# Message passing in graph layers on one Trainium2 core: edge stage with edges as rows, an addition on VectorE and paired transposes

## What is computed

```python
x = layernorm(x + L0(x))   # normalised aggregation, @W, relu
x = layernorm(x + L1(x))   # x @ U.T + segment_sum(x[src], dst) @ V.T, relu
x = layernorm(x + L2(x))   # mean aggregation, concatenated with x, @W
x = layernorm(x + L3(x))
# L3, for every edge (src, dst):
h = relu(concat(x[src], x[dst]) @ W1 + b1)
interaction = h @ W2 + b2
gate = sigmoid(interaction @ Wg + bg)
pooled = segment_sum(interaction * gate, src) / max(count, 1)
```

## Time and profile before

| | us |
|---|---|
| median of 3 runs | 5006.15 (4980.84 to 5015.29) |
| profiled execution, its own time | 5014.18 |
| its span, first to last instruction | 5012.5 |
| PE busy in the span | 4088.1 (82%) |
| DVE busy | 2211.0 (44%) |
| ACT busy | 1761.9 (35%) |
| POOL busy | 1593.1 (32%) |

### The profile page before, as it was taken

The page is one execution under the profiler, slowest core; times in us unless marked ns, Lnnn a source line. Parts: engine busy times, 40 slices in busy tenths (PEclk is TensorE's granted clock), DMA queues, the critical chain, the costliest instruction groups (busy, mean ns, idle before and its releaser), DMA issues.

```text
span 5012.5 us, 126263 instructions
## 1 busy us (share of the span) xinstructions
PE 4088.1 (82%) x39351; PEld 3185.7 (64%) x39352; DVE 2211.0 (44%) x6640; ACT 1761.9 (35%) x3887; POOL 1593.1 (32%) x1694
## 2 busy tenths in 40 slices
PE   6873688888798999968988998788788888897895
PEld 3442344444598989846776776666666776676674
DVE  9998899999604030232222222222222222222224
ACT  7861588888400000122222222222222222222222
POOL 0000100000001010165555555555555555555553
PEclk9985899999899999956567656767777667767767
DMA  1000122222597979611111111111111111111111
GB/s 39 4 2 9 64 112 103 103 103 114 217 346 261 344 264 338 234 37 38 38 38 40 39 40 38 37 39 40 37 39 39 38 40 39 39 40 38 38 41 33
DMA packets 182786, 443.67 MB, mean 89 GB/s; under 512 B 52923, under 2 KB 111555, under 8 KB 176159
## 3 DMA queue, kind: packets, MB, share of 16 engines
q1 hardware_dynamic: 131503, 387.98, 22.4%
q0 software_dynamic: 51040, 53.55, 5.4%
q10 hardware_dynamic: 144, 1.05, 0.1%
HBM read 356.29 MB, written 86.12 MB: 88 GB/s over the span
## 4 chain that ended last, share of the span: by engine, by line
PE 46%; DVE 14%; another core or an unknown queue 12%; issue 10%; ACTq 6%; DMA 6%; ACT 4%; DVEq 1%; POOL 1%; SPq 0%; PEldq 0%; POOLq 0%
PE ps L1528 9%; PE ps L1636 8%; DVE x L542 7%; PE ps L1658 7%; PE ps L1646 7%; PE ps L1633 7%; PE ps L1499 6%; DMA rows<-adjacency 5%; DVE rows L696 3%; ACTq L1334 2%; ACTq L1328 2%; ACTq L1333 2%; ACT stage L1263 1%; PE ps L1418 1%
## 5 line engine op out<-in xcount | busy, mean ns | idle before, releaser
L1057 POOL DMA_INDIRECT x<-b_table,gidx x1568 | 1492.3, 952 | 1307.7 <-ACT x L1336 796.1
L902 DVE TENSOR_TENSOR x<-x,ps 128x256 f32<-128x256 f32 x440 | 185.4, 421 | 1592.5 <-ACT x L1349 1372.2
L1343 ACT ACTIVATE x<-ps,b1col 64x512 f32<-64x512 f32 x440 | 299.0, 679 | 1529.8 <-remote 884.9
L1646 PE MATMUL ps<-w2cat,x 65*128 65x128 f32 x3520 | 705.7, 359 | 100.7 <-ACT x L1343 69.2
L1636 PEld LDWEIGHTS ps<-ident,x 128*64 128x64 f32 x3520 | 617.4, 191 | 200.7 <-issue 168.1
L1646 PEld LDWEIGHTS ps<-w2cat,x 65*128 65x128 f32 x3520 | 597.8, 255 | 220.9 <-issue 156.7
L1499 PE MATMUL ps<-rows 128*128 128x448 bf16 x2272 | 615.8, 399 | 147.9 <-DVE rows L696 69.4
L1658 PE MATMUL ps<-x 128*128 128x65 f32 x3520 | 640.4, 343 | 116.2 <-DVE x L902 96.0
L1528 PE MATMUL ps<-x,rows 128*128 x22050 | 688.9, 194 | 55.6 <-DVEq L783 33.8
L1636 PE MATMUL ps<-ident,x 128*64 128x128 f32 x3520 | 690.6, 358 | 40.8 <-issue 40.6
L1528 PEld LDWEIGHTS ps<-x,rows 128*128 128x128 bf16 x22050 | 670.3, 98 | 74.5 <-issue 65.0
(11 more groups left out here) (270 smaller groups left out, 2279.8 us busy)
## 6 DMA issues: line engine op xcount, KB each, us to landing
rows<-adjacency SPq DMA_DIRECT2D x150, 800.0 KB, 6.2
rows<-adjacency SPq DMA_DIRECT2D x150, 768.0 KB, 6.2
adjacency<-stage SPq DMA_DIRECT2D x50, 1568.0 KB, 5.2
x<-src_rows SPq DMA_DIRECT2D x440, 128.0 KB
x<-b_table,gidx POOLq DMA_INDIRECT x1568
key_rows<-x ACTq DMA_DIRECT2D x1, 1024.0 KB, 4.4
b_table<-AGG SPq DMA_DIRECT2D x1, 1024.0 KB, 5.3
out_dram<-X SPq DMA_DIRECT2D x1, 1024.0 KB
```

What stands on the lines that cost most here:

```text
L1057: e.indirect_dma_start(out=BGT[:, s, j, :], out_offset=None, in_=b_table, in_offset=bass.IndirectOffsetOnAxis(ap=gidx[:, u * G + j:u * G + ...
L1646: ins = e.matmul(ps[:, 2 + u, j * P:(j + 1) * P], H[0:D + 1, u, j * P:(j + 1) * P], w2cat[:], start=True, stop=True)
```

## The change

Two things in the edge stage are computed in another layout, and the loops are put one item deeper.

1. **Edges as rows.** `hidden` on TensorE becomes `edge_rows` (L1657 of the changed kernel) and `turn_rows` (L1668). `edge_rows` takes a piece of `OT` (128 nodes x 128 edges, bf16) as weights and a part of `AT` (64 columns) as the moving side: 4 pieces x 3 parts are 12 bf16 matmuls of 64 columns. The result has the edge on the partition, in bank 6 or 7.
2. **Addition on VectorE.** `add_b` (L896) adds this to `BT`, from PSUM and the local memory, 128 x 256 fp32, written over `BT`.
3. **Paired transposes.** `turn_rows` transposes `BT` in 2 transposes of 128 columns. Each turns two pieces of 128 edges at once, so the features of the first piece lie on partitions 0 to 63 and those of the second on 64 to 127.
4. **Relu** on ScalarE is two instructions of 64 x 256, one for each half of the partitions (L1362). The bias `b1col` is loaded twice, for both halves.
5. **Order.** On TensorE a step of the loop was hidden(i), interact(i-1), sum_edges(i-2). It is now edge_rows(i), turn_rows(i-1), interact(i-2), sum_edges(i-3). On VectorE it was make_hot_t(i), gated(i-2), add_sum(i-3), make_hot(i) and is now add_b(i-2), make_hot_t(i), gated(i-4), add_sum(i-5), make_hot(i-1). On ScalarE it was hidden(i), copy_part(i+2), gate(i-1) and is now hidden(i-1), gate(i-2), copy_part(i+2). Eight items instead of four are written out ahead of the loop.

```diff
+            def add_b(i, s):
+                e.wait_ge(rows_ready, i + 1)
+                e.wait_ge(b_copied, i + 1)
+                e.tensor_tensor(BT[:, s, :], ps[:, 6 + s % 2, 0:G * D], BT[:, s, :], ALU.add).then_inc(b_added, 1)
...
-            with e.Fori(1, ITEMS // 4) as r:
+            with e.Fori(2, ITEMS // 4) as r:
                 for s in range(4):
                     i = 4 * r + s
+                    add_b(i - 2, (s + 2) % 4)
                     make_hot_t(i, r, s, False)
-                    gated(i - 2, s % 2, False)
-                    add_sum(i - 3, (s + 1) % 2)
-                    make_hot(i, s, False)
+                    gated(i - 4, s % 2, False)
+                    add_sum(i - 5, (s + 1) % 2)
+                    make_hot(i - 1, (s + 3) % 4, False)
...
-                e.activation(H[0:D, u, :], ps[0:D, u, :], ACT.Relu, bias=b1col[:, 0:1]).then_inc(h_ready, 1)
+                pair = H[0:D, u, :].rearrange("p (a h n) -> p a h n", h=2, n=P)
+                for h in range(2):
+                    ins = e.activation(pair[:, :, h, :],
+                                       ps[h * D:(h + 1) * D, u, 0:2 * P].rearrange("p (a n) -> p a n", n=P),
+                                       ACT.Relu, bias=b1col[h * D:(h + 1) * D, 0:1])
+                ins.then_inc(h_ready, 1)
...
-                    hidden(i, s % 2, False)
-                    copy_part(i + 2, (s + 2) % 4, False)
-                    gate(i - 1, (s + 1) % 2, False)
+                    hidden(i - 1, (s + 1) % 2, False)
+                    gate(i - 2, s % 2, False)
+                    copy_part(i + 2, (s + 2) % 4, False)
...
-            def hidden(i, s, first):
-
-                u = s % 2
+            def edge_rows(i, s, first):
+
                 e.wait_ge(at_ready, i + 1)
                 e.wait_ge(ot_ready, i + 1)
-                e.wait_ge(b_copied, i + 1)
+                if not first:
+                    e.wait_ge(b_added, i - 1)
+                for j in range(G):
+                    for k in range(3):
+                        ins = e.matmul(ps[:, 6 + s % 2, j * D:(j + 1) * D], OT[:, s % 2, j * P:(j + 1) * P],
+                                       AT[:, s, k * D:(k + 1) * D], start=(k == 0), stop=(k == 2))
+                ins.then_inc(rows_ready, 1)
+
+            def turn_rows(i, s, first):
+
+                e.wait_ge(b_added, i + 1)
                 if not first:
                     e.wait_ge(h_ready, i - 1)
-                for k in range(3):
-                    e.matmul(ps[0:D, u, :], AT[:, s, k * D:(k + 1) * D], OT[:, u, :], start=(k == 0), stop=False,
-                             skip_group_check=True)
-                for j in range(G):
-                    ins = e.matmul(ps[0:D, u, j * P:(j + 1) * P], BT[:, s, j * D:(j + 1) * D], ident[:], start=False,
-                                   stop=(j == G - 1), skip_group_check=True)
+                e.sem_inc(turn_passed, 1)
+                for j in range(G // 2):
+                    ins = e.transpose(ps[:, s % 2, j * P:(j + 1) * P], BT[:, s, j * P:(j + 1) * P], ident[:])
                 ins.then_inc(h_ps_ready, 1)
...
-                    hidden(i, s, False)
-                    interact(i - 1, (s + 1) % 2, False)
-                    sum_edges(i - 2, (s + 2) % 4, False)
+                    edge_rows(i, s, False)
+                    turn_rows(i - 1, (s + 3) % 4, False)
+                    interact(i - 2, s % 2, False)
+                    sum_edges(i - 3, (s + 1) % 4, False)
```

More of the change, by code:

```diff
@@ L384, in build_gnn @@
         h_ps_ready = sem("h_ps_ready")
+        rows_ready = sem("rows_ready")
+        b_added = sem("b_added")
+        turn_passed = sem("turn_passed")
         h_ready = sem("h_ready")
@@ L884, in make_hot_t @@
                 if not first:
-                    e.wait_ge(h_ps_ready, i - 1)
+                    e.wait_ge(rows_ready, i - 1)
                 e.tensor_scalar(OT[:, s % 2, :], SROW[:, s, :], part_f[:, 0:1], None,
                                 ALU.is_equal).then_inc(ot_ready, 1)
+            def add_b(i, s):
+                e.wait_ge(rows_ready, i + 1)
+                e.wait_ge(b_copied, i + 1)
+                e.tensor_tensor(BT[:, s, :], ps[:, 6 + s % 2, 0:G * D], BT[:, s, :], ALU.add).then_inc(b_added, 1)
             def make_hot(i, s, first):
@@ L915, in _ @@
             e.sem_inc(sum_taken, 1)
-            for i in range(4):
-                make_hot_t(i, 0, i, i < 2)
+            for i in range(8):
                 if i >= 2:
[L919 to L922, removed]
-            with e.Fori(1, ITEMS // 4) as r:
+                    add_b(i - 2, (i - 2) % 4)
+                make_hot_t(i, i // 4, i % 4, i < 2)
+                if i >= 4:
+                    gated(i - 4, i % 2, i < 6)
+                if i >= 5:
+                    add_sum(i - 5, (i - 5) % 2)
+                if i >= 1:
+                    make_hot(i - 1, (i - 1) % 4, i < 5)
+            with e.Fori(2, ITEMS // 4) as r:
                 for s in range(4):
                     i = 4 * r + s
+                    add_b(i - 2, (s + 2) % 4)
                     make_hot_t(i, r, s, False)
-                    gated(i - 2, s % 2, False)
-                    add_sum(i - 3, (s + 1) % 2)
-                    make_hot(i, s, False)
+                    gated(i - 4, s % 2, False)
+                    add_sum(i - 5, (s + 1) % 2)
+                    make_hot(i - 1, (s + 3) % 4, False)
+            make_hot(ITEMS - 1, (ITEMS - 1) % 4, False)
             for i in (ITEMS - 2, ITEMS - 1):
+                add_b(i, i % 4)
+            for i in range(ITEMS - 4, ITEMS):
                 gated(i, i % 2, False)
-            for i in range(ITEMS - 3, ITEMS):
-                add_sum(i, i % 2)
+                add_sum(i - 1, (i - 1) % 2)
+            add_sum(ITEMS - 1, (ITEMS - 1) % 2)
             e.wait_ge(sum_taken, ITEMS + 1)
@@ L1354, in _ @@
             copy_part(1, 1, True)
-            for i in range(4):
-                hidden(i, i % 2, i < 2)
+            for i in range(8):
+                if i >= 1:
+                    hidden(i - 1, (i - 1) % 2, i < 3)
+                if i >= 2:
+                    gate(i - 2, i % 2, i < 4)
                 copy_part(i + 2, (i + 2) % 4, i < 2)
-                if i:
-                    gate(i - 1, (i - 1) % 2, i < 3)
-            with e.Fori(1, ITEMS // 4) as rnd:
+            with e.Fori(2, ITEMS // 4) as rnd:
                 for s in range(4):
                     i = 4 * rnd + s
-                    hidden(i, s % 2, False)
+                    hidden(i - 1, (s + 1) % 2, False)
+                    gate(i - 2, s % 2, False)
                     copy_part(i + 2, (s + 2) % 4, False)
-                    gate(i - 1, (s + 1) % 2, False)
-            gate(ITEMS - 1, (ITEMS - 1) % 2, False)
+            hidden(ITEMS - 1, (ITEMS - 1) % 2, False)
+            for i in (ITEMS - 2, ITEMS - 1):
+                gate(i, i % 2, False)
             for half in range(2):
@@ L1662, in _ @@
             e.wait_ge(dve, mark["a_split"])
-            for i in range(4):
-                hidden(i, i, i < 2)
+            for i in range(8):
+                edge_rows(i, i % 4, i < 2)
                 if i >= 1:
-                    interact(i - 1, (i - 1) % 2, i < 3)
+                    turn_rows(i - 1, (i - 1) % 4, i < 3)
                 if i >= 2:
-                    sum_edges(i - 2, i - 2, i < 4)
-            with e.Fori(1, ITEMS // 4) as rnd:
+                    interact(i - 2, i % 2, i < 4)
+                if i >= 3:
+                    sum_edges(i - 3, (i - 3) % 4, i < 5)
+            with e.Fori(2, ITEMS // 4) as rnd:
                 for s in range(4):
                     i = 4 * rnd + s
-                    hidden(i, s, False)
-                    interact(i - 1, (s + 1) % 2, False)
-                    sum_edges(i - 2, (s + 2) % 4, False)
-            interact(ITEMS - 1, (ITEMS - 1) % 2, False)
+                    edge_rows(i, s, False)
+                    turn_rows(i - 1, (s + 3) % 4, False)
+                    interact(i - 2, s % 2, False)
+                    sum_edges(i - 3, (s + 1) % 4, False)
+            turn_rows(ITEMS - 1, (ITEMS - 1) % 4, False)
             for i in (ITEMS - 2, ITEMS - 1):
-                sum_edges(i, i % 4, False)
+                interact(i, i % 2, False)
+                sum_edges(i - 1, (i - 1) % 4, False)
+            sum_edges(ITEMS - 1, (ITEMS - 1) % 4, False)
 _INS = ["x", "src", "dst", "L0_gnn_W", "L0_gnn_b", "L1_gnn_U", "L1_gnn_V", "L2_gnn_W", "L2_gnn_b",
```

6 lines of the change are left out of this document (3 added, 3 removed).

## The result

| | before | changed |
|---|---|---|
| median of 4 runs, us | 5007.65 (4980.84 to 5015.29) | 5060.39 (5056.28 to 5065.32) |
| ratio, 95% interval | | 1.0115 (1.0076 to 1.0155) |
| span of the profiled execution | 5012.5 | 5054.6 |
| granted clock over the span | 0.78 | 0.68 |

The forecast was 4405 us, with a range from 4170 to 4700. The time lies outside it, above its upper end. Slower by over 1% had a chance of 0.06 and no change within 1% had 0.05; the interval of the ratio touches both.

The account below looks back on a forecast made before the run. PE was taken to bound the edge stage, with its results seen late. Savings of 451 us by the chain and 657 by busy time, 702 at most, gave 600 off 5014, less 8: about 4405 us, own range 4330 to 4500.

Parts of the forecast that it names:

- The new work on PE: Edge stage, PE: twelve matmuls and two transposes cost 1.21 us an item at 1.2 GHz, 0.68 at 2.4.
- VectorE and ScalarE: Edge stage: the addition takes 0.42 us on VectorE, hidden; ScalarE's two relus take 0.8 us, 0.12 more.
- floor of about 2.8 us for ScalarE: Edge stage: ScalarE's register loads keep it from going below about 2.8 us an item.
- The sum: Edge stage: 451 us saved by the chain, 657 by busy time, 702 at most; 600 taken, giving about 4405.
- the factor 0.6: Edge stage, PE: share taken as saved of the replaced lines' time, in both the chain and busy-time sums.
- rival 1: Edge stage: clock stays low, PE always busy at 1.2 GHz, no late signals; 702 us saved, 4304; chance 0.15.
- catches up after a late signal: Edge stage: PE with more room makes up for signals seen late; reason for taking 600 us, nearer the upper end.
- rival 5: Edge stage: no change, what delays the signals holds some 6.4 us an item whatever PE does; 5006; chance 0.05.
- Rival 4: Edge stage: slower, PE's 4.82 plus 2.01 us of uncovered late signals, 6.83 an item; about 5190; chance 0.06.
- Rival 3: Edge stage: late signals stay, only 451 us saved, 4555; with a fourth signal up to 4755; chance 0.21.
- rival 2: Edge stage: GpSimd becomes the bound, 1568 gathers at 1.25 us each; 4135 to 4170 us; chance 0.15.
- What would show it: Signs in the edge stage's profile: PE busy near 1700 us instead of 2379, GpSimd's copy waits 796 towards 200.

Follow-up runs that it names:

- experiment 1: Both kernels without the gathers of the edge stage: 4134.65 us for the changed kernel, 3766.07 us for the kernel before, one run each.
- experiment 5: Changed kernel plus four unused bf16 products of 256 columns an item: 4149.05 us with gathers, 3409.21 us without.
- recorded pair: The first timing of the kernel before and the changed kernel, with nothing else altered: 5007.65 and 5060.39 us, ratio 1.0115.
- experiment 3: The changed kernel, unaltered, timed again beside the kernel before: 4154.14 us, ratio 1.0013.
- later runs: Both kernels, unaltered, timed again beside the experiments: about 4150 us for the kernel before, about 4154 us for the changed one.
- experiment 4: Kernel before with plain transfers for gathers: 3766.12 us; with half the gathers: 3765.59; changed kernel with six semaphore increments ahead of each gather: 4179.74.
- experiment 7: Changed kernel with four more 32 KB transfers an item from SyncE: 4156.6 us; changed kernel alone once more: 4153.79 us.

## Why the prediction was wrong, step by step

- **The new work on PE**, said to be 1.21 us an item at 1.2 GHz and 0.68 at 2.4: right and slightly too high. It is 0.64 + 0.48 = 1.12 (experiment 1) and 0.35 + 0.25 = 0.60 (experiment 5). The twelve weight loads cost no more than the dense layers' had shown: 0.053 and 0.029 us an instruction. `interact` fell as well, from 2.01 to 1.71 and from 1.09 to 0.89, without being touched. The item is 4.43 instead of 4.82, and 2.33 instead of 2.61.
- **VectorE and ScalarE**: right. `add_b` takes 420 ns; the pair of relus 2 x 467 = 0.93 us instead of 0.8, inside the bounds. The turn's wait for the addition, 0.16 us an item, is under the 0.3 that was named as a sign of being wrong. The floor of about 2.8 us for ScalarE was hardly too high: experiment 5 without gathers ran at 2.77 an item.
- **The sum** is where it failed, in two terms. First, the factor 0.6 was applied to the busy time at the clock mix of the kernel before, 0.68. The changed form runs at 0.5 throughout, against 0.68. An item that stays at the low level gains, from 6.74 to 4.43; one that goes from the high level to the low one loses, from 3.57 to 4.43. The forecast named this only as rival 1, and there as a gain, since it was counted against 6.74.
- Second, and this is the step that failed in the recorded pair: the saving was put at 600, near the upper end, because a PE with more room "catches up after a late signal". It doesn't. The lateness of the relus grew from 732 to 1085 us, and PE also started fewer instructions late in a run of gathers. PE's idle time grew by the same 305 us by which its work shrank, and the span is 42 us longer. That PE's results are seen late, as read from the earlier trace rows, was right; that a lighter PE would make up for it had no row behind it.
- **The rivals.** The period of an item in the profile after is (5010.8 - 2184.1) / 439 = 6.44 us, from the relus in experiment 3; before it was 6.42. So rival 5 (0.05) is nearest in the number: "what delays the signals holds the stage to some 6.4 us an item whatever PE does". Rival 4 (0.06) priced PE at 1.2 GHz with 2.01 us of late time uncovered. With the measured 4.43 its sum is 6.44 as well. That it meets to the last digit is partly luck: the relus' "remote" wait after is 804 / 440 = 1.83 us. And the reason that it gave, turn, addition and relu hanging on each other, shows in only 138 of PE's 748 us of idle time. The two rivals can't be told apart by these runs. Rival 3 let the late time grow by up to 200 us for a fourth signal of PE, 4755 at most; it grew by more. In the later runs it is rival 2: GpSimd waits for nothing, 4154 against the 4135 to 4170 that it gave. But the kernel before is there too, 4150, so the change is worth nothing. Of rival 1 the sign came, clock 0.5 in every slice of the stage, but not the gain.
- **What would show it**: PE busy near 1700 us was said, 2074 came; waits of GpSimd for the copies were to shrink from 796 to 200, they are 900 in the recorded profile and 8 in the later one; "the clock falls while PE also idles" was named as what would make the forecast wrong, and that is what came.

**The gain, then, went three ways.** The clock took it back: at equal clock the changed form is 1.24 us an item cheaper, at its own it is 0.86 dearer than the kernel before at full clock (shown by experiments 1 and 5). GpSimd's gathers at 1.26 us hide whatever is left (experiments 3, 4). And in the recorded pair PE's signals came late and its starts thinned out, by as much time as the change had saved; that is seen in the traces, and its cause isn't shown.

**What stays open.** Why PE's signals are late and its starts few in the recorded pair, and not in any later run. Whether the gathers have a part in it isn't shown, since all runs with fewer gathers fell where the delay was absent. Nor is it known whether it belongs to a chip, to that hour or to something else. The gathers themselves were alike: a median of 947 ns against 944, and the same spacing of 1.25. More traffic doesn't bring it (experiment 7). That the changed form suffers more may come from its 60 instructions an item on PE and its weight loads, against 54; that is argued, not shown. Whether a higher clock would have helped there couldn't be tried, since the condition didn't come back. Nor is it shown which property of the new form holds the clock down, only that it isn't the transposes alone and that wide products beside them lift it. No version was found that beats both whole kernels; it would need fewer or cheaper gathers first.

## What to carry to other kernels

Before costing a cut on TensorE, write the path out at each clock level, and ask at which the new form will run. Here, without gathers, the new form stayed at 1.2 GHz, busy without a gap, and cost 4.43 us an item against 3.57 for the old form at 2.4. Look for the engine that has the same total whatever you do (here GpSimd, 1568 x 1.26 us) and run both kernels without its work: that shows in two runs what the change is worth and what hides it. Idle time put down to "remote" or "issue" isn't free room: as long as its cause is unknown, give the case that it grows a price and a chance. And time the kernel before once more beside each experiment; only this showed that the recorded pair was a level of its own.

## What was unexpected of the hardware

- Four unused bf16 products of 256 columns an item, in the changed kernel without gathers, brought the granted clock from 0.50 to 1.00 in a stage in which PE was busy without a gap either way, and the time from 4135 to 3409 us.
- A fp32 transpose through PE costs half of the product with the identity that gives the same: 0.24 against 0.50 us at 1.2 GHz.
- The eight instructions of `interact`, alike in both kernels, took 2.01 us at 1.2 GHz behind the identity products with their 64-column weights and 1.71 behind the transposes (1.09 and 0.89 at 2.4). Why isn't shown.
- The same two kernels took 5007 and 5060 us in one set of runs and 4150 and 4154 in all others; in the first, PE's starts in the changed kernel fell from between 6.0 and 7.4 per us to about 1 after 8 us of gathers back to back, and 162 of 440 relus began over 1.5 us after PE's work for them was over by the model; in the later run none did.
